# Order of score, value, turn and projection work within a step of three attentions of a decoder kernel

## Chip, cores and metric

One Trainium2 chip, one core. The metric is the device time of one execution in microseconds (us), the median of several runs; lower is better.

## What is computed

A decoder of four layers works on x of 16 sequences, 128 tokens, 256 features, all in f32. Each layer adds an attention-like, a cross-attention-like and a feed-forward part to x. Three of the attentions are touched by the change: `l1a` (layer 1, causal self-attention), `l2fa` (the self-attention without mask inside layer 2's feed-forward part) and `l3x` (layer 3, cross-attention to a context, with a time bias, 4 key and value heads). They all have 16 query heads of 16 features. The one of layer 3, cut to what matters:

```python
q = (query @ Wq).reshape(B, S, H, D).transpose(0, 2, 1, 3)
k = (key @ Wk).reshape(B, S, G, D).transpose(0, 2, 1, 3)
v = (value @ Wv).reshape(B, S, G, D).transpose(0, 2, 1, 3)
scores = jnp.einsum('bhqd,bhkd->bhqk', q, k_rep) * SCALE
...
scores = scores + time_bias[:, None, :, :]
...
w = jax.nn.softmax(scores, axis=-1)
out = jnp.einsum('bhqk,bhkd->bhqd', w, v_rep)
return out.transpose(0, 2, 1, 3).reshape(B, S, E) @ Wo
```

## The kernel before

Every attention of the kernel is built by one function, `attention_block` (from L393 on). Its plan says which mask it has, how many heads, and where keys and values come from. The order of work on each engine is written out by hand; the engines meet through semaphores.

**Steps.** The work is cut into T = 32 steps t: step t handles 8 of the 16 heads (HEADS = 8, in two groups of UNIT = 4) of one sequence, so two steps make a sequence and four (PER = 4) make a pair of sequences. What belongs to one step is spread over the following ones: its scores come in step t, its exponentials and maxima too, its sums one step later, the turning (transposing) of its probabilities TURN = 3 steps later, its value products VALUES = 4 steps later, and the output projection of a whole sequence in the step after the second half's value products.

**Projections.** Beside this, the projections for the next pair run as "fills" of two PSUM banks, `proj`: y (the turned rows of x), c (the turned context, in cross-attentions), k, q, v and, for each sequence, o (the output projection). A table `at[(t, sec)]` deals them out over the steps and over three sections of each step. In l1a and l2fa the first step of a round of four has y, the second k, the third q, the fourth v, all in section 0, and o in section 1 of the first and third. In l3x the first has c in section 0 and o and y in section 2, the second k and the third q in section 1 (with o in section 2 of the third), the fourth v in section 0. I call the four steps r0 to r3. A fill waits until its bank has been emptied of the fill two before it.

**TensorE** (the loop at L726 to L741). `score(t)` (L659) multiplies queries with a wide key tile in which each head has its own columns; it waits until the first group's exponentials of step t-1 are done, because there are three score banks for two in use. In l1a and l0x a mask matmul stands ahead of it (L675). `turn(t - TURN)` (L693) makes eight transposes, and waits for the probabilities and for the copies of the half turned a step before. `values(t - VALUES)` (L702) makes eight products of 32 columns each, and waits for both copies of its turned probabilities (`copied[0]` by VectorE, `copied[1]` by ScalarE) and for the copy out of the value products before it. Where `adjacent` (L415) is set, as it is for l2a and l0x, the values follow directly behind the scores; elsewhere, so in the three attentions of the change, they stand between sections 1 and 2. The turn stands between sections 0 and 1.

**VectorE** (L910 to L944), in each step: two row maxima (L904, or L901 with the addend in l3x), the sums of the step before (L921) and their reciprocals (L927), the emptying of section 0's fills, the copy of the first turned half (L937), the emptying of sections 1 and 2. Emptying k takes eight operations (L809) in l1a, l0x and l2fa. Emptying o adds it to the residual and takes that sequence's statistics (L856 to L862).

**ScalarE** (L1081 to L1112), in each step: four exponentials (L1070), the emptying of section 0, four exponentials (in l2fa and l3x the second four also sum, L1072), the copy of the second turned half (L1096), section 1, the copy out of the value products (L1079; directly behind the first four exponentials where `adjacent`), section 2. It empties y, c and part of q, k, v; in l3x also k, in eight operations (L1029).

**GpSimd** multiplies the probabilities by the reciprocals (L994) and normalises the next rows. **SyncE** loads the context and masks.

After step T a "head" is made: the first four sequences' rows of the next block are normalised by VectorE (L279), turned by TensorE (L289) and copied (L299, L308), between the last turns and value products.

Of the kernel before, what the change touches and what calls it, by code (L numbers as in the profile page):

```python
# [389 lines left out]
UNIT = 4  # L390


def attention_block(chip, plan, w, prefetch, have_stats, leave_twice):  # L393
# [18 lines left out]
    VB = 3 if small or S == 1 else 2  # L412
    added = plan.mask == "timebias" or t_ in ("l2a",)
    between = added and not small and not ctxsrc
    adjacent = t_ in ("l2a", "l0x")  # L415
    SUMMED = UNIT if t_ in ("l3x", "l2fa") else HEADS


# [52 lines left out]
    with ExitStack() as scope:  # L471
# [101 lines left out]
        with nc.Block() as block:  # L573
# [29 lines left out]
            def _(pe):  # L603
# [122 lines left out]
                for t in range(T + VALUES + 2):  # L726
                    if t < T:
                        score(t)
                    if adjacent and 0 <= t - VALUES < T:
                        values(t - VALUES)  # L730
                    for x in at[(t, 0)]:
                        project(x)
                    if 0 <= t - TURN < T:
                        turn(t - TURN)
                    for x in at[(t, 1)]:
                        project(x)
                    if not adjacent and 0 <= t - VALUES < T:
                        values(t - VALUES)
                    for x in at[(t, 2)]:
                        project(x)  # L740
                    if t == T + 1 and head:  # L741
                        pe.wait_ge(exps_done, 2 * T)
                        head.turn(pe, scores)
# [25 lines left out]
            def _(dve):  # L769
# [119 lines left out]
                if plan.mask == "timebias":  # L889
                    dve.wait_ge(key_ready, 1)  # L890
                    biased(0)

                def row_max(t, a):
                    b = t // S
                    g, j = divmod(b, PAIR)
                    bank = scores[(2 * t + a) % 3][:, :].rearrange("p (i k) -> p i k", i=UNIT)
                    dve.wait_ge(scores_ready, 2 * t + a + 1)
                    if added:
                        addend = {"timebias": lambda: bias[:, b, :], "causal": lambda: chip.causal[:, :], "support": lambda: mask_b[:, g % 2, j, :]}[plan.mask]()
                        for i in range(UNIT):  # L900
                            op = dve.tensor_tensor_reduce(out=bank[:, i, :], in0=bank[:, i, :], in1=addend, scale=-1.0, scalar=FMAX, op0=ALU.add, op1=ALU.min,  # L901
                                                          accum_out=nmx[:, t % 2, a * UNIT + i:a * UNIT + i + 1])
                    else:
                        op = dve.tensor_reduce(nmx[:, t % 2, a * UNIT:(a + 1) * UNIT], bank, AX.X, ALU.max, negate=True)  # L904
                    if plan.mask == "support":
                        dve.drain()
                        op = dve.tensor_scalar(nmx[:, t % 2, a * UNIT:(a + 1) * UNIT], nmx[:, t % 2, a * UNIT:(a + 1) * UNIT], padcol[:, b:b + 1], None, ALU.min)
                    op.then_inc(max_ready, 1)

                for t in range(T + VALUES + 2):  # L910
                    if t < T:
                        row_max(t, 0)
                        if between:
                            for x in at[(t, 0)]:
                                if not by_scalar(x[1]):
                                    empty(x)
                        row_max(t, 1)
                    if 0 <= t - 1 < T:
                        u = t - 1
                        dve.wait_ge(exps_done, 2 * u + 2)  # L920
                        dve.tensor_reduce(rsum[:, u % 2, 0:SUMMED], p[:, u % (TURN + 1), 0:SUMMED, :], AX.X, ALU.add)  # L921
                        dve.drain()
                        if plan.mask == "support":
                            dve.wait_ge(pads_done, u + 1)
                            dve.scalar_tensor_tensor(out=rsum[:, u % 2, :], in0=padt[:, u % 2, :], scalar=npad[:, u // S:u // S + 1], in1=rsum[:, u % 2, :], op0=ALU.mult, op1=ALU.add)
                            dve.drain()
                        dve.reciprocal(rinv[:, u % (TURN + 1), :], rsum[:, u % 2, :]).then_inc(rinv_ready, 1)  # L927
                    if plan.mask == "keymask" and t % PER == 0 and t // PER + 1 < PAIRS:
                        make_valid(t // PER + 1)
                    for sec in range(3):  # L930
                        for x in at[(t, sec)]:
                            if not by_scalar(x[1]) and not (between and sec == 0 and t < T):
                                empty(x)
                        if sec == 0 and 0 <= t - TURN < T:
                            u = t - TURN
                            dve.wait_ge(probsT_ready, 2 * u + 1)
                            dve.tensor_copy(pT[:, u % 2, 0:UNIT, :], probsT[0][:, :].rearrange("p (i q) -> p i q", i=UNIT)).then_inc(copied[0], 1)  # L937
                    if plan.mask == "timebias" and 1 <= t < NB // 4:
                        biased(t)
                    if t == T and head:  # L940
# [61 lines left out]
            def _(act):  # L1002
# [78 lines left out]
                for t in range(T + VALUES + 2):  # L1081
# [2 lines left out]
                    if adjacent and 0 <= t - VALUES < T:  # L1084
                        copy_out(t - VALUES)
                    for x in at[(t, 0)]:
                        if by_scalar(x[1]):
                            empty(x)
                    if t < T:
                        exps(t, 1)  # L1090
# [2 lines left out]
                    if 0 <= t - TURN < T:  # L1093
                        u = t - TURN
                        act.wait_ge(probsT_ready, 2 * u + 2)
                        act.copy(pT[:, u % 2, UNIT:HEADS, :], probsT[1][:, :].rearrange("p (i q) -> p i q", i=UNIT)).then_inc(copied[1], 1)  # L1096
                    for x in at[(t, 1)]:
                        if by_scalar(x[1]):
                            empty(x)
                    if not adjacent and 0 <= t - VALUES < T:  # L1100
# [3312 lines left out]
```

## Time and profile before

| | |
|---|---|
| Median of 3 runs | 2851.52 us (2845.75 to 2853.3) |
| Profiled execution, its own time | 2852.58 us |
| Its span | 2850.7 us |
| Mean granted TensorE clock | 0.949 |
| TensorE busy | 2524.3 us, 89% of the span |
| VectorE busy | 1729.2 us, 61% |
| ScalarE busy | 1257.8 us, 44% |
| GpSimd busy | 856.2 us, 30% |
| First and last scores of l1a | 582.6 and 737.8 us |
| First and last scores of l2fa | 1721.5 and 1864.8 us |
| First and last scores of l3x | 2268.8 and 2416.1 us |

The time of an execution lies about 2 us above its span, from the first to the last instruction. The shares are means over the whole kernel; a single attention looks different, so the rows below are taken inside single rounds of four steps. In the timeline, PE is TensorE, DVE VectorE, ACT ScalarE and POOL GpSimd. A PE row's length has the modelled end of its last matmul in it, so the time that a group takes from TensorE's queue is read from its start to the start of the next group.

### The profile page before, as it was taken

The numbers are of one execution on the slowest core, as the hardware profiler recorded it, in microseconds if no ns is written. First come the engines' busy times: TensorE is split into PE (matmuls) and PEld (weight loads), VectorE is DVE, ScalarE is ACT, GpSimd is POOL, SyncE is SP. The second block draws the span as 40 slices with busy tenths as digits, with TensorE's granted clock in tenths as the row PEclk, the third lists the DMA queues.
The fourth block names the chain that finished last, engine by engine and source line by source line (L and its number), as shares of the span: only waits on it lengthen the run. The fifth ranks groups of instructions, "written<-read, shape, count | busy, mean of one in ns | idle before, by whom it ended". The sixth has DMA issues, their size and how long they took to land. (4 is left out here: it accounts for less than half of the span.)

```text
span 2850.7 us, 49404 instructions
## 1 busy us (share of the span) xinstructions
PE 2524.3 (89%) x16337; PEld 1828.8 (64%) x16337; DVE 1729.2 (61%) x4957; ACT 1257.8 (44%) x3451; POOL 856.2 (30%) x687
## 2 busy tenths in 40 slices
PE   4998989989799889599998998969969899969997
PEld 2666765766544356477776776748956576449996
DVE  7875986588766644355564567973345588344443
ACT  2333664256455323444443445734432488324342
POOL 4533540045431044122221226631110044132222
PEclk8999999999899899799999999979989999989999
DMA  9001000000300333200001002051130300531110
GB/s 321 15 0 51 14 2 18 1 16 1 84 11 1 58 94 116 96 1 1 1 1 47 18 1 75 2 207 35 39 90 1 87 19 2 192 121 50 53 51 27
DMA packets 155271, 144.08 MB, mean 51 GB/s; under 512 B 62024, under 2 KB 139982, under 8 KB 154640
## 3 DMA queue, kind: packets, MB, share of 16 engines
q1 hardware_dynamic: 142880, 112.17, 13.6%
q0 software_dynamic: 10560, 27.19, 2.8%
q8 instruction: 137, 2.24, 0.3%
q10 hardware_dynamic: 1584, 1.57, 0.2%
q14 instruction: 110, 0.90, 0.1%
HBM read 99.70 MB, written 43.02 MB: 50 GB/s over the span
## 5 line engine op out<-in xcount | busy, mean ns | idle before, releaser
L994 POOL TENSOR_TENSOR room<-room 128x1024 f32<-128x1024 f32 x144 | 273.9, 1902 | 408.7 <-DVE room L927 408.5
L1473 PE MATMUL l3f_out<-room,Y 128*128 x624 | 141.1, 379 | 0.0
L921 DVE TENSOR_REDUCE room<-room 128x8 f32<-128x1024 f32 (+1 forms) x144 | 139.9, 972 | 1.0 <-ACT room L1072 0.8
L3645 DVE SCALAR_TENSOR_TENSOR room<-l1x_v,room 128x512 f32<-128x512 f32 x128 | 86.8, 685 | 65.5 <-ACT room L3791 65.2
L994 POOL TENSOR_TENSOR room<-room,Y 128x1024 f32<-128x1024 f32 x32 | 60.7, 1896 | 215.3 <-DVE Y L927 215.3
L1473 PEld LDWEIGHTS l3f_out<-room,Y 128*128 128x128 f32 x624 | 115.6, 190 | 14.2
L1070 ACT ACTIVATE room<-l2a_scores,Y 128x128 f32<-128x128 f32 x256 | 73.4, 375 | 96.6 <-DVE Y L901 96.6
L3791 ACT ACTIVATE room<-l1x_u 128x512 f32<-128x512 f32 x128 | 76.0, 598 | 76.0 <-PE l1x_v L3460 75.7
L1070 ACT ACTIVATE room<-l0x_scores,room 128x128 f32<-128x128 f32 x256 | 74.0, 390 | 55.0 <-DVE room L904 55.0
L1070 ACT ACTIVATE room<-l1a_scores,room 128x128 f32<-128x128 f32 x256 | 71.6, 387 | 59.4 <-DVE room L904 59.4
L626 PE MATMUL l2a_proj<-room 128*128 128x256 f32 x384 | 90.7, 384 | 0.0
L955 POOL MEMSET room<- 128x3072 f32 (+1 forms) x4 | 9.4, 2338 | 269.9 <-POOLq L144 269.9
L1775 DVE SCALAR_TENSOR_TENSOR Y<-Y,vecs 128x256 f32<-128x256 f32 x39 | 18.9, 485 | 116.6 <-DMA Y<-out,l3f_dest 116.6
L901 DVE CUSTOM_DVE_ANT_0 l2a_scores<-l2a_scores,causal 128x128 f32<-128x128 f32 x256 | 65.7, 323 | 33.0 <-PE l2a_scores L688 32.9
L1473 PE MATMUL l2fm_out<-room,Y 128*128 x368 | 83.1, 379 | 0.0
L1866 ACT COPY l3f_yn<-room 128x2048 f32 x39 | 74.5, 1911 | 16.4 <-DMA sorted_rows<-l3f_yn,l3f_place_i 16.0
L1463 PEld LDWEIGHTS l3f_hidden<-Y,l3f_yn 128*128 128x128 f32 x640 | 75.5, 196 | 5.8 <-DVE Y L1728 5.3
L1463 PE MATMUL l3f_hidden<-Y,l3f_yn 128*128 128x128 f32 x640 | 77.8, 281 | 1.2 <-DVE Y L1728 1.1
L626 PEld LDWEIGHTS l2a_proj<-room 128*128 128x128 f32 x384 | 70.5, 190 | 11.5 <-issue 3.1
L1911 POOL DMA_INDIRECT out<-Y,l3f_dest x39 | 39.1, 1002 | 127.5 <-DVE Y L1775 127.5
L1463 PEld LDWEIGHTS l3f_hiddenT<-Y,l3f_yn 128*128 128x128 f32 x608 | 69.7, 192 | 6.4 <-DVE Y L1728 5.8
L1473 PEld LDWEIGHTS l2fm_out<-room,Y 128*128 128x128 f32 x368 | 68.2, 190 | 8.4
(878 smaller groups left out, 6939.5 us busy)
## 6 DMA issues: line engine op xcount, KB each, us to landing
sorted_rows<-head SPq DMA_DIRECT2D x1, 16640.0 KB, 57.2
room<-in_L_ffn_w SPq DMA_DIRECT2D x16, 1024.0 KB, 13.3
room<-in_L_ffn_W SPq DMA_DIRECT2D x16, 1024.0 KB, 12.5
room<-in_ctx SPq DMA_DIRECT2D x32, 256.0 KB, 3.1
Y<-sorted_rows SPq DMA_DIRECT2D x62, 130.0 KB, 2.1
room<-sorted_rows SPq DMA_DIRECT2D x39, 130.0 KB, 2.1
room<-results SPq DMA_DIRECT2D x8, 512.0 KB, 7.4
room<-in_L_ffn_routed_w SPq DMA_DIRECT2D x4, 512.0 KB
```

What stands on the lines that cost most here:

```text
L626: mm = pe.matmul(bank[:, (c - i) * PT:(c - i + 1) * PT], w.v[kind][:, kc, c * P:(c + 1) * P], (y_of(g) if kind == "q" else c_of(g))[:, kc, ...
L901: op = dve.tensor_tensor_reduce(out=bank[:, i, :], in0=bank[:, i, :], in1=addend, scale=-1.0, scalar=FMAX, op0=ALU.add, op1=ALU.min, accum ...
L921: dve.tensor_reduce(rsum[:, u % 2, 0:SUMMED], p[:, u % (TURN + 1), 0:SUMMED, :], AX.X, ALU.add)
L994: pool.tensor_tensor(p[:, u % (TURN + 1), :, :], p[:, u % (TURN + 1), :, :], rinv[:, u % (TURN + 1), :].unsqueeze(2).to_broadcast([P, HEAD ...
L1070: op = act.activation(p[:, t % (TURN + 1), h, :], bank[:, i * P:(i + 1) * P], ACT.Exp, bias=nmx[:, t % 2, h:h + 1], scale=sign)
L1463: mm = pe.matmul(hidden[n % 2][a][:, q * P:(q + 1) * P], stage[:, n % 2, kc * F + f * P:kc * F + (f + 1) * P], rowsT[:, n % 2, kc, :], sta ...
L1473: mm = pe.matmul(obank[n % 2][:, 0:D], hT[:, n % 2, f, :], chip.room[:, bass.ds(at + (SLOT // 2 + f * D), D)], start=(f == 0), stop=(f == ...
L1775: op = dve.scalar_tensor_tensor(out=result[:, n % 2, :], in0=result[:, n % 2, :], scalar=gate[:, n % 2, 0:1], in1=so_far, op0=ALU.mult, op ...
L1866: act.copy(stage[:, n % 2, :], chip.room[:, bass.ds(at, KC * F)]).then_inc(staged, 1)
L1911: pool.indirect_dma_start(final_rows, bass.IndirectOffsetOnAxis(dest[:, n % DESTS:n % DESTS + 1], 0), result[:, n % 2, :], None, bounds_ch ...
L3645: dve.scalar_tensor_tensor(out=W[:, k % 2, p, :], in0=v_bank[n % 2][:, :], scalar=0.0, in1=W[:, k % 2, p, :], op0=ALU.max, op1=ALU.min).th ...
L3791: act.activation(W[:, k % 2, p, :], u_bank[n % 2][:, :], ACT.Relu).then_inc(u_ready, 1)
```

## The change

A new flag, `turn_first`, is set for l1a, l2fa and l3x, and sets `adjacent` for them. A step on TensorE is then: scores, value products, turn, and the fills of sections 0, 1 and 2. VectorE's copy of the first turned half becomes a small function, `copy_turned`; with the flag it stands behind the second row maxima and ahead of the sums. On ScalarE the copy out of the value products moves behind the first four exponentials, and the emptying of section 0 moves behind the copy of the second turned half. The other attentions keep their order.

```diff
--- before.py
+++ after.py
@@ -412,7 +412,8 @@
     VB = 3 if small or S == 1 else 2
     added = plan.mask == "timebias" or t_ in ("l2a",)
     between = added and not small and not ctxsrc
-    adjacent = t_ in ("l2a", "l0x")
+    turn_first = t_ in ("l1a", "l2fa", "l3x")
+    adjacent = turn_first or t_ in ("l2a", "l0x")
     SUMMED = UNIT if t_ in ("l3x", "l2fa") else HEADS
 
 
@@ -728,9 +729,11 @@
                         score(t)
                     if adjacent and 0 <= t - VALUES < T:
                         values(t - VALUES)
+                    if turn_first and 0 <= t - TURN < T:
+                        turn(t - TURN)
                     for x in at[(t, 0)]:
                         project(x)
-                    if 0 <= t - TURN < T:
+                    if not turn_first and 0 <= t - TURN < T:
                         turn(t - TURN)
                     for x in at[(t, 1)]:
                         project(x)
@@ -890,6 +893,10 @@
                     dve.wait_ge(key_ready, 1)
                     biased(0)
 
+                def copy_turned(u):
+                    dve.wait_ge(probsT_ready, 2 * u + 1)
+                    dve.tensor_copy(pT[:, u % 2, 0:UNIT, :], probsT[0][:, :].rearrange("p (i q) -> p i q", i=UNIT)).then_inc(copied[0], 1)
+
                 def row_max(t, a):
                     b = t // S
                     g, j = divmod(b, PAIR)
@@ -915,6 +922,8 @@
                                 if not by_scalar(x[1]):
                                     empty(x)
                         row_max(t, 1)
+                    if turn_first and 0 <= t - TURN < T:
+                        copy_turned(t - TURN)
                     if 0 <= t - 1 < T:
                         u = t - 1
                         dve.wait_ge(exps_done, 2 * u + 2)
@@ -931,10 +940,8 @@
                         for x in at[(t, sec)]:
                             if not by_scalar(x[1]) and not (between and sec == 0 and t < T):
                                 empty(x)
-                        if sec == 0 and 0 <= t - TURN < T:
-                            u = t - TURN
-                            dve.wait_ge(probsT_ready, 2 * u + 1)
-                            dve.tensor_copy(pT[:, u % 2, 0:UNIT, :], probsT[0][:, :].rearrange("p (i q) -> p i q", i=UNIT)).then_inc(copied[0], 1)
+                        if sec == 0 and not turn_first and 0 <= t - TURN < T:
+                            copy_turned(t - TURN)
                     if plan.mask == "timebias" and 1 <= t < NB // 4:
                         biased(t)
                     if t == T and head:
@@ -1084,7 +1091,7 @@
                     if adjacent and 0 <= t - VALUES < T:
                         copy_out(t - VALUES)
                     for x in at[(t, 0)]:
-                        if by_scalar(x[1]):
+                        if by_scalar(x[1]) and not turn_first:
                             empty(x)
                     if t < T:
                         exps(t, 1)
@@ -1094,7 +1101,7 @@
                         u = t - TURN
                         act.wait_ge(probsT_ready, 2 * u + 2)
                         act.copy(pT[:, u % 2, UNIT:HEADS, :], probsT[1][:, :].rearrange("p (i q) -> p i q", i=UNIT)).then_inc(copied[1], 1)
-                    for x in at[(t, 1)]:
+                    for x in (at[(t, 0)] if turn_first else []) + at[(t, 1)]:
                         if by_scalar(x[1]):
                             empty(x)
                     if not adjacent and 0 <= t - VALUES < T:
```

## Rows read from the trace of the kernel before

**Rows 1.** Busy time in one round of four steps: l0x, l1a, l2fa, l3x.

```profile
core 0: us, PE busy (x) PEld busy (x) DVE busy (x) ACT busy (x) POOL busy (x), PEclk, DMA share, GB/s
318.37:338.76 20.39, 20.38 (x177) 14.99 (x176) 18.97 (x38) 12.92 (x45) 10.78 (x8) 1.00 0.07 16
626.22:646.84 20.62, 20.48 (x173) 14.34 (x173) 18.74 (x37) 12.72 (x45) 10.85 (x8) 1.00 0.01 1
1783.45:1801.93 18.48, 18.33 (x168) 13.90 (x164) 16.62 (x37) 14.21 (x61) 12.90 (x10) 1.00 0.01 2
2331.98:2350.95 18.97, 18.14 (x170) 13.68 (x169) 15.99 (x88) 17.07 (x69) 9.67 (x7) 1.00 0.05 16
```

**Rows 2.** Timeline, l1a, TensorE in r2: start us, length us, engine, what.

```profile
652.88 1.99 PE L626 MATMUL l1a_proj<-room 128*128 128x256 f32 x8
...
655.01 1.07 PE L699 MATMUL l1a_probsT<-ident,room 128*128 128x128 f32 x8
...
655.91 1.03 PE L648 MATMUL l1a_proj<-room 128*128 128x256 f32 x4
...
656.87 0.64 PE L717 MATMUL l1a_out<-room 128*32 128x128 f32 x16
```

**Rows 3.** Timeline, l0x, from the end of r1 to the values of r3.

```profile
322.66 0.59 PE L675 MATMUL l0x_scores<-l0x_mask_b,ident_b 128*128 128x512 bf16 x2
...
322.87 3.71 DVE L809 TENSOR_SCALAR room<-l0x_proj,vecs,block_of 128x256 f32<-128x256 f32 x8
...
323.19 1.13 PE L681 MATMUL l0x_scores<-room 64*128 64x256 f32 x8
...
324.25 0.65 PE L717 MATMUL l0x_out<-room 128*32 128x128 f32 x16
...
325.76 1.03 PE L648 MATMUL l0x_proj<-room 128*128 128x256 f32 x4
...
326.50 1.27 DVE L904 TENSOR_REDUCE room<-l0x_scores 128x4 f32<-128x512 f32 x2
...
326.63 1.99 PE L626 MATMUL l0x_proj<-room 128*128 128x256 f32 x8
...
327.20 1.14 ACT L1070 ACTIVATE room<-l0x_scores,room 128x128 f32<-128x128 f32 x4 [4.13 <-DVE room L904]
...
328.37 1.18 ACT L1070 ACTIVATE room<-l0x_scores,room 128x128 f32<-128x128 f32 x4
...
328.46 0.59 PE L675 MATMUL l0x_scores<-l0x_mask_b,ident_b 128*128 128x512 bf16 x2
...
329.38 0.65 ACT L1096 COPY room<-l0x_probsT 128x512 f32<-128x512 f32 x1
...
330.12 0.64 PE L717 MATMUL l0x_out<-room 128*32 128x128 f32 x16
```

**Rows 4.** Timeline, l3x, TensorE and ScalarE from r1 to r3.

```profile
2337.14 3.10 ACT L1029 ACTIVATE room<-l3x_proj,block_of 128x256 f32<-128x256 f32 x8
...
2340.53 0.65 PE L717 MATMUL l3x_out<-room 128*32 128x128 f32 x16 [0.27 <-ACT room L1079]
...
2341.11 1.13 PE L648 MATMUL l3x_proj<-room 128*128 128x256 f32 x4
...
2342.17 1.14 PE L681 MATMUL l3x_scores<-room 64*128 64x256 f32 x8
...
2343.86 1.10 PE L634 MATMUL l3x_proj<-room 128*128 128x64 f32 x8 [0.56 <-ACT room L1041]
...
2344.49 1.14 ACT L1070 ACTIVATE room<-l3x_scores,room 128x128 f32<-128x128 f32 x4 [0.53 <-DVE room L901]
```

**Rows 5.** Timeline, l2fa: second exponentials, ScalarE's copy, VectorE's emptying of k.

```profile
1793.31 0.40 ACT L1072 ACTIVATE room<-l2fa_scores,room 128x128 f32<-128x128 f32 x1
...
1794.68 0.65 ACT L1096 COPY room<-l2fa_probsT 128x512 f32<-128x512 f32 x1
...
1805.18 3.65 DVE L809 TENSOR_SCALAR room<-l2fa_proj,vecs,block_of 128x256 f32<-128x256 f32 x8
```

**Rows 6.** Timeline, l1a, tail: VectorE's copy of a turned half.

```profile
748.29 0.68 DVE L937 COPY room<-l1a_probsT 128x512 f32<-128x512 f32 x1
```

## The prediction

> **What bounds the kernel now.** I read the windows first: one full round of four steps in each of the three attentions, and one of l0x, which already runs its value products directly behind the scores and is left as it is. A step is one half (8 of 16 heads) of one sequence, and four steps carry one projection round for the next pair of sequences. In l1a TensorE is busy 20.48 of 20.62 us, in l2fa 18.33 of 18.48, in l3x 18.14 of 18.97; the granted clock is 1.00 in all four [rows 1]. So TensorE's queue sets the pace, but VectorE is at 18.74 of 20.62 in l1a and ScalarE at 17.07 of 18.97 in l3x: neither has much room. What I then look for in the timelines is only two things: which pair of neighbours on TensorE's queue costs time, and how early each copy is ready that TensorE waits for.
>
> In l1a's third step the queue loses time to VectorE: the q fill begins at 652.88 and the turn behind it at 655.01, 2.13 us later [rows 2], where the same fill in l0x takes 326.63 to 328.46, 1.83 us [rows 3]. The turn waited for VectorE's copy of the half turned before, which stood behind the eight operations that empty the k fill. A second loss is the order itself: the output projection ahead of the values takes 655.91 to 656.87, 0.96 us [rows 2], and 0.87 ahead of another full-width fill (325.76 to 326.63) [rows 3].
>
> **The change in parts.** Nothing is added or removed: 32 steps in each attention, with the same matmuls, copies and DMAs; SP's and GpSimd's queues are as they were. On TensorE values(t-4) moves from behind the first or second group of projections to directly behind score(t), turn(t-3) follows it, and all fills come last. VectorE's copy of the turned half moves ahead of the sums and of the emptying; the change's description says "directly behind the sums", but in the diff it stands directly behind the row maxima, ahead of the sums. ScalarE copies the value products out between its two groups of exponentials, and empties all fills behind its copy of the turned half. Steps 0 to 2 have no turn or values, steps 28 to 31 no fills but the output projection, so the change acts on six full rounds (steps 4 to 27) of each attention, on four steps after them and on the tail.
>
> *Floor of TensorE, l1a.* l0x has the order wanted, the same mask matmul and one more fill, the context's four transposes, which I take at 0.49 us (as long as half an output projection's 0.87, and a little more). Its round is 20.39 us [rows 1]; less 0.49 that is 19.9. Both losses above are gone in it: 0.30 for the copy, some 0.1 a step for the values.
>
> *Does a copy come late in l1a?* This is what the new order risks: the k fill now comes last in its step, so VectorE empties it later, and values(t-4) needs, right behind the scores, copies that were made one step before instead of having a whole step of slack. I count from the start of step r1 (the one with k), by l0x's rows [rows 3]: mask 0.53 (322.66 to 323.19), scores 1.06 (to 324.25), values and turn 1.51 (to 325.76), k 1.8: 4.9, and VectorE starts at about 5.0 (in l0x it starts 0.21 behind the end of the fill, 322.87 against 322.66). The eight operations take 3.63 (to 326.50), so the row maxima of r2 start at 8.6; exponentials 0.70 later (327.20), 1.17 for four and the copy out (to 328.37), 1.01 for the other four (to 329.38), and values may start 0.74 behind the start of ScalarE's copy (330.12): 12.2. TensorE gets there at 4.9 + (0.53 + 1.06 + 1.51 + 1.83 + 0.87 = 5.8) + 1.59 = 12.3. So l1a just fits: 19.9 against 20.62, 0.7 a round, **-4.3 us** over six. Bounds: VectorE's 18.74 of busy time leaves only 1.2 a round free, so 0 if it uses that up in waits; -5.5 if the late fills also save the 0.1 that l0x pays where q is followed by the mask.
>
> *l2fa.* No mask: the floor is 19.9 less four times 0.53, and plus 0.09 in each step, because the scores (which use 64 rows) now follow full-width work: in l3x an output projection that stands between values and scores takes 1.06 (2341.11 to 2342.17) [rows 4], two such boundaries, against the 0.96 with one and the 0.87 with none. That gives 18.14. Here the copies do come late. ScalarE's second four exponentials also sum and take 1.37 us (1793.31 to the copy at 1794.68) [rows 5], not 1.01, and TensorE arrives earlier because there is no mask. From r1: 1.06 + 1.51 + 1.83 = 4.4, k emptied from 4.5 for 3.63, row maxima at 8.13, then 0.70 + 1.17 + 1.37 + 0.74 = 12.1. TensorE is ready for the values of r3 at 4.4 + (1.06 + 1.51 + 1.83 + 0.96 = 5.36) + 1.06 = 10.8. **Stall 1.3 us in every round**: 19.44 against 18.48, **+5.8 us** over six. Today this does not show, since k is filled before the turn (VectorE takes it up at 1805.18, 3.2 us into the step that starts at 1801.93) [rows 1, 5] and the values stand at the end of the step. Bounds: -2 (no stall) to +8 (a second stall of 0.4 where y is emptied).
>
> *l3x.* Floor: 18.14, plus 0.49 for the context, less 0.89 because its v fill is half as long (1.10 us against 1.99) [rows 4, 3]: 17.75. Two waits of today go: 0.27 for the copy out (2340.53) and 0.56 for ScalarE ahead of v (2343.86) [rows 4]. But k is emptied by ScalarE: exponentials begin 2.32 behind the scores' start (2342.17, 2344.49) [rows 4], then 1.17 + 1.37 + 0.5 for its copy = 5.3, k for 3.0 (the eight at 2337.14 take 3.10, the end of the last beside what follows) = 8.3, exponentials of r2 1.17 + 1.37 = 10.9, values at 11.6 where TensorE is ready at 10.8: 0.8 lost, and some 0.3 in the step behind it. 17.75 + 1.1 is 18.85; with the round's other overlaps I take 18.7 against 18.97, **-1.5 us** over six. Bounds: -7.3 (floor) to +3.
>
> *Last steps and tails.* In steps 28 to 31 the chain scores, maxima, exponentials, copy, values, turn closes in two steps; with l2fa's sums that is 0.5 us longer than today. In step 32 VectorE now waits for a turn that stands behind the values before it takes the last sums, and the rows of the next block's head wait for it; in l1a the copy at 748.29 [rows 6] already waits behind that work. I take 0.5 us each, bounds -0.5 and +2: **+1.5** and **+0.5**.
>
> **Sum.** -4.3 + 5.8 - 1.5 + 0.5 + 1.5 = +2.0. The profiled execution took 2852.58 us (span 2850.7); 2854.6 for one like it. The median of the three runs is 1.1 below that, so I predict 2853.5. Differences under 0.3% (8.6 us) can't be told from none with this kernel.
>
> A page of the Trainium skill bears on the order. "TensorEngine Tiling (Array Packing)", section Key Properties, says that a change of tiling mode drains TensorE. The trace has such a price: the 0.96 against 0.87 above. By the rule alone l1a has three changes of mode a step instead of four (full, 64 rows, 32 columns, full), l2fa three as before, and l3x one less in one step of four.
>
> **Rivals.**
> *A, the order on TensorE alone counts.* One boundary less in l1a at 0.09 (0.96 less 0.87) [rows 2, 3] for 29 steps, one in seven steps of l3x, no stall won or lost elsewhere: -3.2, 2848.3, no change that can be told. Against it speaks the late copy in l2fa, for it that 0.09 is plain in the rows. The skill's rule named above would have it so. Chance 0.12.
> *B, faster.* The copies are never late: every round runs at TensorE's floor, 19.9, 18.14 and 17.75, so -4.3, -2.0 and -7.3, 2838. It decides at ScalarE's copy in r2: it must start by 10.1 us after r1's start in l2fa where I count 11.4. For it: today TensorE waits for a copy in these rounds only 0.3 to 0.6 us at a time. Against it: the 3.63 of emptying k is one block that nothing passes. Chance 0.14.
> *C, slower.* VectorE's copy, now ahead of the sums, waits for a turn that is itself held behind the values. With 0.5 us of that in one step of each round, and VectorE's 1.2 free in l1a gone, l1a's round is 21.1 (+3.0), l2fa's 19.9 (+8.8), l3x's as today, and each tail costs 1.2 (+3.6): about +15, 2867. It decides where the turn's first half comes later than the end of the row maxima. By l0x's rows the first half is done some three quarters through the 1.51 us of values and turn, 2.7 after the mask, and the two maxima, 1.27 long, end near 3: close enough to be possible [rows 3]. Chance 0.16.
> *D, the copy is not where the description has it.* Behind the sums it would come later by one sum; l0x has it there, and its values in r3 start at 330.12 with ScalarE's copy ready at the same moment. That is under 0.1 us a round: it changes no number here. It is no case of its own.
>
> **How the numbers follow.** My forecast has 0.58: with A that is 0.70 for no change, of which 0.01 each goes to either side for its spread: faster 0.15, same 0.68, slower 0.17. The range of the forecast by its bounds is 2846 to 2861. To leave out no more than 2 in 10 it reaches into B and C: 2843 to 2864.
>
> **What would show it.** In the profile after: l1a's round near 19.9 with the wait of the turn for VectorE gone; l2fa's near 19.4 with a wait of over 1 us ahead of the values in one step of four, put down to ScalarE's or VectorE's copy; l3x's near 18.7 with two shorter ones, and the waits ahead of v and for the copy out gone; granted clock still 1.00. If l2fa's values never wait, B holds and my chain from k to the copy is wrong. If VectorE shows idle time ahead of its copy of the turned half, it is C.

## The result and the profile after

The changed kernel takes 2869.17 us in the median of five runs (2862.58 to 2873.74); the kernel before, in the same session, 2851.52 (2845.37 to 2855.61, five runs). The ratio is 1.0064, with a 95% interval of 1.0046 to 1.0081: 0.6% slower, outside the range that I gave. The one profiled execution took 2862.58 us (span 2860.8), the lowest of the five.

The busy time in one round of four steps, in the same order as in [rows 1], here of the changed kernel (stretch and its length, then busy us and instructions of each engine, granted clock, DMA):

```profile
core 0: us, PE busy (x) PEld busy (x) DVE busy (x) ACT busy (x) POOL busy (x), PEclk, DMA share, GB/s
319.40:339.79 20.39, 20.39 (x177) 14.99 (x176) 18.96 (x38) 12.88 (x45) 10.78 (x8) 1.00 0.07 16
626.62:646.53 19.91, 19.86 (x173) 14.49 (x172) 18.83 (x38) 12.48 (x44) 10.86 (x7) 1.00 0.00 1
1780.52:1800.06 19.54, 18.21 (x165) 13.82 (x164) 16.93 (x36) 14.21 (x61) 12.93 (x9) 1.00 0.01 2
2341.48:2362.09 20.61, 17.97 (x169) 13.79 (x168) 16.17 (x86) 17.09 (x67) 9.66 (x7) 1.00 0.05 14
```

l0x, which the change leaves alone, is the same to 0.01 us. l1a's round fell from 20.62 to 19.91, l2fa's rose from 18.48 to 19.54, and l3x's from 18.97 to 20.61. In both that rose TensorE does slightly less busy time than before and waits for the rest.

From trace to trace the same round of the same code repeats to some 0.04 us, while executions of one kernel differ by 10 us, so I judge by rounds, and by the time from the start of an attention's first fill to the end of its last one. The exception is l3x's first round, which took 19.35, 19.46 and 20.39 us in three traces of the old order.

| | before | after | difference | forecast |
|---|---|---|---|---|
| l1a, steps 4 to 27 | 123.2 | 119.0 | -4.2 | -4.3 |
| l2fa, steps 4 to 27 | 110.0 | 117.3 | +7.3 | +5.8 |
| l3x, steps 4 to 27 | 114.4 | 123.5 | +9.1 | -1.5 |
| first fill to last fill: l1a | 181.0 | 177.9 | -3.1 | |
| the same, l2fa | 167.2 | 178.8 | +11.6 | |
| the same, l3x | 182.1 | 191.0 | +8.8 | |

The last three rows sum to +17.3, and the medians differ by 17.7. The two profiled executions differ by 10 only because the untouched rest of the kernel took some 7 us less in the second.

**l2fa.** The timeline of the changed kernel from r1 to r3 (start us, length us, engine, line, what, and idle time before it; lines of other engines between them are left out):

```profile
1785.16 3.71 DVE L812 TENSOR_SCALAR room<-l2fa_proj,vecs,block_of 128x256 f32<-128x256 f32 x8 [0.61 <-PE l2fa_proj L627]
...
1788.78 1.27 DVE L911 TENSOR_REDUCE room<-l2fa_scores 128x4 f32<-128x512 f32 x2
...
1789.49 1.14 ACT L1077 ACTIVATE room<-l2fa_scores,room 128x128 f32<-128x128 f32 x4 [3.81 <-DVE room L911]
...
1790.69 1.13 PE L682 MATMUL l2fa_scores<-room 64*128 64x256 f32 x8 [0.32 <-ACT room L1077]
...
1792.03 0.64 ACT L1103 COPY room<-l2fa_probsT 128x512 f32<-128x512 f32 x1
...
1792.77 0.64 PE L718 MATMUL l2fa_out<-room 128*32 128x128 f32 x16 [0.95 <-issue]
```

k is emptied from 4.64 us after the start of its step (1780.52), row maxima at 8.26, ScalarE's copy at 11.51, values at 12.25. This is the chain of the forecast, where I had 4.5, 8.13, 11.4 and 12.1. ScalarE was idle for 3.81 us in front of its exponentials: not its load is the trouble but what it waits for. The scores of r3 wait 0.32 us and its values 0.95, together 1.27 where I had a stall of 1.3.

The first of the six rounds is another case. It has no output projection in r0, and in the kernel before it took 17.61 us for that. Now it takes 19.55 like the others: TensorE waits 0.93 us ahead of r1's values, which start 5.17 us behind the scores of r0 (1737.46 to 1742.63), with no emptying of k between them. r0 is only 3.10 us long there.

**l3x.** What I had not seen stands in r0:

```profile
2360.33 0.64 ACT L1103 COPY room<-l3x_probsT 128x512 f32<-128x512 f32 x1
2360.80 0.66 ACT L1027 COPY room<-l3x_proj 128x512 f32<-128x512 f32 x1
...
2361.51 0.66 PE L617 MATMUL l3x_proj<-ident,room 128*128 128x128 f32 x4 [1.36 <-ACT room L1027]
2362.09 1.14 PE L682 MATMUL l3x_scores<-room 64*128 64x256 f32 x8
2362.20 0.59 ACT L1025 COPY room<-l3x_proj 128x512 f32<-128x512 f32 x1 [0.75 <-PE l3x_proj L617]
```

r0 has three fills, c, o and y, for two banks. y needs the bank of c. ScalarE now empties c (L1027) behind its second exponentials and its copy, and the three fills have moved together, so TensorE stands for 1.36 us ahead of y (L617). In the same round it also waits ahead of the values in two steps:

```profile
PEld l3x_proj L617 <- ACT room L1027: 1.8, 1, 1.8
PE l3x_proj L617 <- ACT room L1027: 1.4, 1, 1.4
PE l3x_out L718 <- issue: 0.7, 1, 0.7
PE l3x_out L718 <- ACT room L1103: 0.6, 1, 0.6
```

(In the round from 2355.49 to 2376.10: engine, line and what it waited for; us in all, times, longest.) The two waits of before, for the copy out and ahead of v [rows 4], are gone.

**The tail of l2fa** grew from 16.1 us (start of the last scores to the end of the last fill) to 19.7. ScalarE's copy, TensorE's values and VectorE's copy and sums in step 32, of the changed kernel:

```profile
1870.71 0.64 ACT L1103 COPY room<-l2fa_probsT 128x512 f32<-128x512 f32 x1
...
1871.60 0.64 PE L718 MATMUL l2fa_out<-room 128*32 128x128 f32 x16 [2.76 <-ACT room L1103]
1872.18 1.09 PE L700 MATMUL l2fa_probsT<-ident,room 128*128 128x128 f32 x8
...
1872.87 0.69 DVE L898 COPY room<-l2fa_probsT 128x512 f32<-128x512 f32 x1 [2.67 <-PE l2fa_probsT L700]
...
1873.48 0.68 DVE L930 TENSOR_REDUCE room<-room 128x4 f32<-128x512 f32 x1
```

and the same sums in the kernel before:

```profile
1868.35 0.63 ACT L1096 COPY room<-l2fa_probsT 128x512 f32<-128x512 f32 x1
1868.53 0.69 DVE L921 TENSOR_REDUCE room<-room 128x4 f32<-128x512 f32 x1 [0.59 <-ACT room L1072]
```

They stood 0.18 us behind the start of ScalarE's copy and stand 2.77 behind it now. TensorE's mean granted clock in this tail was 1.00 before and 0.91 after, and its busy time, for the same work, 12.18 us and 13.69: 1.5 of the 3.6 us go with the clock.

### The profile page after: what moved, and what is told of

Its sections match the earlier page's. It is cut to its first block and busy times, and to the rows that moved or that the text cites. A ratio compares the mean times of both kernels' runs of the same rounds, so it can differ in the third digit from the quotient of the medians.

```text
span 2860.8 us, 49404 instructions
## 1 busy us (share of the span) xinstructions
PE 2507.7 (88%) x16337; PEld 1824.1 (64%) x16337; DVE 1735.5 (61%) x4957; ACT 1254.1 (44%) x3451; POOL 856.1 (30%) x687
## 5 line engine op out<-in xcount | busy, mean ns | idle before, releaser
L1782 DVE SCALAR_TENSOR_TENSOR Y<-Y,vecs 128x256 f32<-128x256 f32 x39 | 18.9, 484 | 104.0 <-DMA Y<-out,l3f_dest 104.0
L908 DVE CUSTOM_DVE_ANT_0 l3x_scores<-l3x_scores,room 128x128 f32<-128x128 f32 x256 | 64.9, 325 | 22.3 <-PE l3x_scores L682 21.9
```

Source lines behind the costliest of these rows:

```text
L1782: op = dve.scalar_tensor_tensor(out=result[:, n % 2, :], in0=result[:, n % 2, :], scalar=gate[:, n % 2, 0:1], in1=so_far, op0=ALU.mult, op ...
```

## The experiments

Times of whole kernels are compared with the kernel before on the same chip; one chip was 13 us slower for the kernel before. Experiments 3 to 7, 9 and 10 were executed once each, so I judge them by their rounds and not by their whole times.

**1. The new order in l1a alone.**

```diff
-    turn_first = t_ in ("l1a", "l2fa", "l3x")
+    turn_first = t_ in ("l1a",)
```

> The new order in l1a alone; l2fa and l3x as in the kernel before. Theory 1 (each attention pays for its own late copy or late bank, independently): l1a takes 178.0 us from its first fill to its last, as in the changed kernel (181.0 before), a round of four steps 19.9; l2fa and l3x are back at 167.3 and 182.2; the whole kernel 3 us under the kernel before, 2848. Theory 2 (the loss is something common to the three, such as the order of VectorE's queue or TensorE's clock): l1a's gain comes and goes with the others, and the total is not under the kernel before.

l1a: rounds of 19.91 or 19.92, but for the first (19.27) and the fifth (20.09), 179.5 us from first fill to last (one early step went slower, in l0x too). l2fa is back at 167.3, l3x at 181.0. Twelve runs: median 2861.56 against 2864.61, ratio 0.9993 (0.9981 to 1.0005). The attentions pay independently, as theory 1 has it. The 3 us cannot be told from none in the whole kernel's time.

**2. c emptied between the exponentials in l3x.**

```diff
                     for x in at[(t, 0)]:
-                        if by_scalar(x[1]) and not turn_first:
+                        if by_scalar(x[1]) and (not turn_first or t_ == "l3x"):
                             empty(x)
...
-                    for x in (at[(t, 0)] if turn_first else []) + at[(t, 1)]:
+                    for x in (at[(t, 0)] if turn_first and t_ != "l3x" else []) + at[(t, 1)]:
```

> The changed kernel, but in l3x ScalarE empties the fill of section 0 (the turned context, c) between its two groups of exponentials, as before the change. Theory 1 (l3x loses because TensorE's y fill waits for the bank that c leaves, 1.36 us in the first step of each round): that wait goes, l3x's round falls from 20.61 to 19.2 to 19.4, the attention from 191.0 to about 182 to 183, the kernel by about 8.5 against the changed one, to some 2860. Theory 2 (l3x loses through the late emptying of k and the late copies that values wait for, as predicted): the round stays at 20.3 or more.

A round of l3x, and TensorE's waits in it:

```profile
2383.32:2402.37 19.05, 17.78 (x170) 13.79 (x169) 16.17 (x87) 17.09 (x68) 9.62 (x6) 1.00 0.01 2
```

```profile
PE l3x_out L718 <- issue: 0.7, 2, 0.5
PE l3x_out L718 <- ACT room L1103: 0.5, 1, 0.5
```

The wait ahead of y is gone, and the last two rounds are 19.05 and 19.06; the first took 20.82, the three behind it 19.53, 19.39 and 19.23. l3x takes 183.8 us instead of 191.0, a little over the 182 to 183 that was expected: the bank of c cost 1.56 us in a late round, and 6.4 over all six. Ratio to the kernel before 1.0025 (1.001 to 1.004), against 1.0064 for the whole change. Theory 1 holds, with a rest of 1.2 us of waits ahead of the values.

**3. VectorE's copy behind the sums**, where the description has it: the two lines of the call stand behind the reciprocal.

```diff
                         row_max(t, 1)
-                    if turn_first and 0 <= t - TURN < T:
-                        copy_turned(t - TURN)
                     if 0 <= t - 1 < T:
...
+                    if turn_first and 0 <= t - TURN < T:
+                        copy_turned(t - TURN)
```

> The changed kernel with VectorE's copy of the turned half behind the sums and reciprocals instead of ahead of them. Theory 1 (the place of this copy matters little inside the rounds, and something in the tail, where the last sums wait behind a turn that waits for the values): rounds of l1a, l2fa and l3x stay at 19.9, 19.5 and 20.6 within 0.15; each tail (step 32 on) is shorter by 1 to 2 us, so 3 to 5 us in all. Theory 2 (VectorE waits for the turn in its new place, and this makes the loss): rounds of l2fa and l3x fall by 0.5 us or more.

Rounds of 19.92, 19.56 and 20.65: nothing moved, and theory 2 falls. Theory 1's 3 to 5 us in the tails did not come either. The tails (last scores to last fill), with TensorE's busy time and granted clock in them:

| | changed kernel | copy behind the sums |
|---|---|---|
| l1a | 18.66, busy 13.69, clock 0.91 | 19.88, busy 15.25, clock 0.83 |
| l2fa | 19.69, busy 13.69, clock 0.91 | 17.11, busy 12.07, clock 1.00 |
| l3x | 19.30, busy 13.73, clock 0.91 | 18.96, busy 13.69, clock 0.91 |

Most of what moves here goes with the clock. In five more runs with the copy ahead of the sums and a clock of 0.91 l2fa's tail took 18.5 to 19.0 us; in experiment 7, which has this copy behind the sums too, it took 18.2 at 0.91. So with like clocks the copy's place is worth 0.3 to 0.8 us in l2fa (1.5 against the changed kernel's own trace) and 0.3 in l3x; whether it also brings the clock down is open.

**4. In l2fa, r3 in the old order** on all engines (scores, v, turn, values; TensorE's part shown).

```diff
+    old_order = lambda t: t_ in ('l2fa',) and t % PER in (3,)
...
-                    if adjacent and 0 <= t - VALUES < T:
+                    old = old_order(t)
+                    if adjacent and not old and 0 <= t - VALUES < T:
                         values(t - VALUES)
-                    if turn_first and 0 <= t - TURN < T:
+                    if turn_first and not old and 0 <= t - TURN < T:
                         turn(t - TURN)
...
```

> The changed kernel, but in l2fa the fourth step of each round (the one with v) keeps the old order on all engines: scores, v, turn, values, copy out late. Theory 1 (l2fa loses because the values of this step wait for copies made late behind the emptying of k): the wait of 0.95 us and more goes, the round falls from 19.54 to 18.3 to 18.5, the attention from 178.8 to about 171 to 172. Theory 2 (it loses by the order itself, the scores of 64 rows behind full-width fills, or by late copies in every step): the round stays over 19.2.

The round rose to 20.30, where theory 1 had 18.3 to 18.5. TensorE's waits in one of them:

```profile
PE l2fa_proj L636 <- ACT room L1049: 1.7, 1, 1.7
PE l2fa_scores L683 <- ACT room L1080: 0.3, 1, 0.3
```

v, now directly behind the scores, waits 1.7 us for its bank, which q holds until ScalarE is behind its late exponentials. A miss that neither theory had: it tells them apart no better than before, but it is the wait for a bank once more, in another attention.

**5. Half of k's emptying left out in l2fa.**

```diff
                     if kind == "k" and small:
-                        for c in range(i, i + per_bank):
+                        for c in range(i, i + (1 if t_ == "l2fa" and g >= 2 else per_bank)):
```

> The changed kernel, but in l2fa VectorE empties only four of the eight parts of each k fill from the third pair of sequences on, so that heads 8 to 15 keep the keys of an earlier pair: that part of the work is left out. Theory 1 (l2fa's loss is the chain from the late k fill over VectorE's 3.6 us of emptying to the copies that the values wait for): the chain is 1.8 us shorter, more than the wait of about 1.3 us, so l2fa's round falls from 19.55 to 18.1 to 18.3, under the 18.48 of the kernel before. Theory 2 (the loss is in the order on TensorE, or in copies that are late in every step): the round falls by less than 0.5.

```profile
1811.23:1829.37 18.14, 18.13 (x166) 13.82 (x165) 15.19 (x32) 14.31 (x62) 12.86 (x10) 1.00 0.01 2
```

18.14 in all six rounds. In five of them TensorE is busy for all but 0.01 to 0.07 us of it. The matmuls and their order are unchanged; only VectorE's block of 3.6 us is 1.8 shorter. So in these five l2fa's whole loss is that block in front of the copies, and 18.14 is the floor that I had worked out from l0x. In the first, which has one output projection less, TensorE is busy for 17.21 us and the wait of 0.93 ahead of r1's values is still there: that one is not k's.

**6. k emptied by ScalarE in l2fa.**

```diff
-                return kind == "q" or (kind == "k" and plan.mask == "timebias")
+                return kind == "q" or (kind == "k" and (plan.mask == "timebias" or t_ == "l2fa"))
```

> The changed kernel, but in l2fa ScalarE empties the k fills, as it does in l3x; VectorE is free of them. Theory 1, by the same chain: ScalarE is through with its copy at 5.4 us after the start of the step with k, with k at 8.3, its exponentials and copy bring the values of r3 to 11.6 instead of 12.2, where TensorE is ready at 10.9: round 18.8 to 19.0 instead of 19.55. Theory 2 (VectorE is what is overloaded in this attention): with 3.6 us of 17 taken from it the round falls to TensorE's floor, 18.2.

The round is 19.24, above the 18.8 to 19.0 that the chain gave, and far from 18.2: with VectorE 3.5 us a round less busy (13.50 against 17.00), the values still wait 0.9 us in one step. VectorE's load is not the bound; that the same block on another engine stands in the same chain fits this, and the chain came out 0.2 to 0.4 short.

**7. The early values alone**: values and copy out directly behind the scores, turn and copies where they were.

```diff
-    turn_first = t_ in ("l1a", "l2fa", "l3x")
-    adjacent = turn_first or t_ in ("l2a", "l0x")
+    turn_first = False
+    adjacent = t_ in ("l1a", "l2fa", "l3x", "l2a", "l0x")
```

> One part of the change alone: in the three attentions the value products and their copy out stand directly behind the scores, but the turn stays behind the fills of section 0, VectorE's copy behind the emptying of section 0, and ScalarE empties section 0 between its exponentials. Theory 1 (the values can stand there only if the copies come early): in l1a and l2fa the copy of r1 now stands behind the emptying of k and the values of r2 wait some 2 us for it: rounds of 21.5 or more in l1a (19.91 with the whole change) and 20.3 or more in l2fa (19.55); in l3x, where ScalarE empties k and the c fill leaves its bank early, 19.0 to 19.4 (20.62). Theory 2 (the early values are the gain and the early turn is the loss): l1a stays at 20.0 or less, l2fa falls to 18.5.

Rounds: l1a 23.7 to 24.0 (21.80 in the first), l2fa 23.4 to 23.5 (21.85 in two), l3x 18.9 to 19.6. The whole kernel took 2902.89 us. One round each of l1a, l2fa and l3x, and TensorE around the wait in l1a:

```profile
695.64:719.62 23.98, 21.58 (x173) 15.83 (x173) 19.12 (x37) 12.82 (x44) 10.85 (x8) 0.93 0.00 1
1855.71:1879.24 23.53, 20.03 (x165) 15.13 (x165) 16.98 (x37) 14.61 (x61) 12.88 (x10) 0.93 0.01 2
2418.05:2437.02 18.97, 17.82 (x169) 13.83 (x168) 16.06 (x88) 17.12 (x70) 9.70 (x7) 1.00 0.01 2
```

```profile
704.91 1.14 PE L682 MATMUL l1a_scores<-room 64*128 64x256 f32 x8
708.44 0.71 PE L718 MATMUL l1a_out<-room 128*32 128x128 f32 x16 [2.40 <-DVE room L898]
709.08 3.35 PE L627 MATMUL l1a_proj<-room 128*128 128x256 f32 x7
```

The wait of 2.4 us is the one expected: VectorE's copy behind the emptying of k. (The last row ends with its window; the whole fill, eight matmuls, takes 3.57 us.) So in l1a the early values alone only lose, and need the early turn and the early copy; the early turn alone was not tried, the early copy alone only in l2fa (experiment 11). In l3x the early values alone are as good as before the change.

**8. l1a alone, and there VectorE's copy behind the sums from step 32 on.**

```diff
-                    if turn_first and 0 <= t - TURN < T:
+                    if turn_first and t < T and 0 <= t - TURN < T:
                         copy_turned(t - TURN)
...
+                    if turn_first and t >= T and 0 <= t - TURN < T:
+                        copy_turned(t - TURN)
```

> The new order in l1a alone, and there VectorE's copy of the turned half behind the sums from step 32 on. Theory 1 (the last sums need not wait for a turn that stands behind the values): l1a's loop stays at 150.25 to 151.5 us, its tail is 0.5 to 1.2 us shorter than the 18.4 to 18.7 of the same order without this; the kernel 3 to 4 us under the kernel before, ratio 0.9985 to 0.9995. Theory 2 (the tail is set by the head's rows and the granted clock): the tail stays within 0.3 us.

l1a's tail is 18.15 us against 18.34 with experiment 1, both at a clock of 0.91; ratio 1.0001 (0.9989 to 1.0013). Theory 2's 0.3 us holds here; experiment 1's 0.9993 and this 1.0001 are one result, no change that can be told.

**9. l3x with c between the exponentials and half of k's emptying left out on ScalarE** (experiment 2's edit and this one).

```diff
                     elif kind == "k" and small:
-                        for c in range(i, i + per_bank):
+                        for c in range(i, i + (1 if t_ == "l3x" and g >= 2 else per_bank)):
```

> The changed kernel with two edits in l3x: ScalarE empties c between its two groups of exponentials, as before, and from the third pair on it empties only four of the eight parts of each k fill (heads 8 to 15 keep an earlier pair's keys: that part of the work is left out). Theory 1 (behind the bank of c, l3x has a second cost of the same kind as l2fa: copies made late behind the emptying of k, now on ScalarE): the round falls from 19.06 to 17.6 to 18.2, near TensorE's floor of 17.6 to 17.8. Theory 2 (with the bank wait gone l3x is at its floor, and 19.06 is TensorE's own work in this order): it stays over 18.8.

The round stays at 19.07 (from the third on; the first took 22.68). Theory 1 is wrong here, and so is theory 2's floor: TensorE still waits, elsewhere. The timeline from r3's scores to r0's values:

```profile
2357.05 1.13 PE L682 MATMUL l3x_scores<-room 64*128 64x256 f32 x8
...
2358.27 0.28 DVE L908 CUSTOM_DVE_ANT_0 l3x_scores<-l3x_scores,room 128x128 f32<-128x128 f32 x1
...
2359.38 1.14 ACT L1077 ACTIVATE room<-l3x_scores,room 128x128 f32<-128x128 f32 x4 [1.60 <-DVE room L908]
...
2360.67 1.13 PE L682 MATMUL l3x_scores<-room 64*128 64x256 f32 x8
...
2361.93 0.64 ACT L1103 COPY room<-l3x_probsT 128x512 f32<-128x512 f32 x1
...
2362.82 0.65 PE L718 MATMUL l3x_out<-room 128*32 128x128 f32 x16 [1.01 <-ACT room L1103]
```

The wait ahead of r3's values is gone and that ahead of r0's has grown to 1.01 us. ScalarE is on time with k. From r3's scores (2357.05) over maxima, exponentials and copy to the values of the next step it takes 5.77 us, and r3, with its short v fill, is only 3.62 long with 1.06 of scores behind it. So the late k decides in which of the two steps TensorE waits, and not how long in both together. It is the wait of l2fa's first round once more.

**10. l3x with c between the exponentials, and VectorE sums all heads.**

```diff
-    SUMMED = UNIT if t_ in ("l3x", "l2fa") else HEADS
+    SUMMED = UNIT if t_ in ("l2fa",) else HEADS
```

> The changed kernel, c emptied between the exponentials in l3x, and there VectorE sums all eight heads, so that ScalarE's second four exponentials take 1.0 us instead of 1.4; the result is the same. Theory 1 (with values directly behind scores, each step of l3x must be at least as long as the chain from its scores over row maxima, exponentials and ScalarE's copy to the next values, 5.6 to 5.8 us less the 1.06 of the next scores, so that short steps are padded to 4.6): the chain is 0.37 shorter in every step, and the round falls from 19.06 to 18.3 to 18.7. Theory 2 (VectorE, busy 16.2 of 19, becomes the bound when it takes over the sums): the round stays at 19.0 or rises.

The last three rounds are 18.85 to 18.87 (the first took 23.75), 0.2 less than 19.06: between the theories. The chain is shorter, but VectorE, now 17.97 of 18.85 busy, takes back part of it, and a wait of 0.2 us for c's bank returns. That a short step is padded up to the chain fits this and experiment 9; how the 1.2 us divide is open.

**11. What the experiments point to**: the new order where it pays, and the two waits of TensorE in the other two shortened in the old order. In l2fa VectorE copies ahead of emptying k in r1; in l3x the v fill stands behind the turn, so that its bank is free.

```diff
-    turn_first = t_ in ("l1a", "l2fa", "l3x")
+    turn_first = t_ in ("l1a",)
...
-... if n * 3 * PER // len(body) == r * 3 + sec and ...
+... if n * 3 * PER // len(body) + (t_ == "l3x" and f[0] == "v") == r * 3 + sec and ...
...
+                    early_copy = t_ == "l2fa" and t % PER == 1 and 0 <= t - TURN < T
+                    if early_copy:
+                        copy_turned(t - TURN)
...
-                        if sec == 0 and not turn_first and 0 <= t - TURN < T:
+                        if sec == 0 and not turn_first and not early_copy and 0 <= t - TURN < T:
                             copy_turned(t - TURN)
```

> The new order in l1a alone, and two small edits in the old order of the others: in l2fa, in the step with k, VectorE copies the turned half ahead of emptying k (the turn of the next step no longer waits for it), and in l3x the v fill stands behind the turn instead of directly behind the scores (its bank is free by then). Theory 1 (waits of TensorE for a late copy or a late bank are what is left to win, and each is worth what the trace shows): l1a's round 19.91, l2fa's 18.1 to 18.2 instead of 18.48, l3x's 18.3 to 18.5 instead of 18.97; l1a 178 to 179.5 us, l2fa 165.5, l3x 178 to 179; the kernel 7 to 9 us under the kernel before, ratio 0.9965 to 0.998. Theory 2 (such waits move on to the next instruction): l2fa and l3x stay within 0.1 of 18.48 and 18.97 a round, the ratio at 0.999 or more.

```profile
1817.66:1835.80 18.14, 18.14 (x169) 13.98 (x165) 16.64 (x38) 14.15 (x62) 12.89 (x10) 1.00 0.01 2
2364.99:2383.65 18.66, 18.30 (x169) 13.75 (x169) 15.86 (x87) 16.99 (x69) 9.63 (x6) 1.00 0.01 2
```

l1a 19.91, l2fa 18.14, l3x 18.66 a round (18.3 to 18.5 was forecast). l2fa takes 166.1 us and l3x 180.6 (165.5 and 178 to 179 were forecast). Eleven runs: 2844.6 against 2852.47 us, ratio 0.9972 (0.9958 to 0.9986). It beats both kernels, the changed one by 0.9% if the two ratios are divided.

## Why the prediction was wrong

**l1a: right.** "19.9 against 20.62", by the round of l0x less the context; measured 19.91, and -4.2 for -4.3. "12.2 against 12.3" was close: in the round from 641.61 r3's values start 12.28 us after r1 (646.01 to 658.29), 0.13 later than directly behind the scores.

**l2fa: right in mechanism, small in size.** I had 19.44 and +5.8; it is 19.54 and +7.3. Experiment 5 shows the chain and the floor of 18.14 to be as worked out. What was missing: the first of the six rounds took 17.61 before, not 18.48, and lost 1.9 instead of 1.1 us, because its short r0 is stretched by the chain from r0's scores to r1's values. I had followed that chain only behind k.

**l3x: the step that failed.** I had -1.5; it is +9.1. "17.75 + 1.1 is 18.85; with the round's other overlaps I take 18.7". I counted when ScalarE is through with k and with its copies, and not when it is through with c, though the change moves that very operation behind the second exponentials, and though a fill waits until its bank has been emptied of the fill two before it. With three fills in r0 and all of them together at the end of the step, y follows c too soon. That is 1.56 us in a late round (experiment 2). Without it the round is 19.06, still 0.4 over my 18.7; leaving out half of k does not shorten it, so the late k of my chain does not set it; the trace of experiment 9 shows a short step stretched to the chain of 5.77 us instead. l3x's rounds make 10.6 of the 15 us by which the forecast of +2.0 fell short.

**Last steps and tails: +2.0 forecast.** In the loop's last steps l2fa lost 0.7 and l3x 0.5. l2fa's tail lost 3.6 where I had 0.5 and a bound of 2; l1a's lost 1.1, l3x's gained 1.0. The order of the waits was as I had it, but I had not followed the chain of copy, values, turn, copy and sums step by step, and I had no term for the clock. In l2fa's tail the clock makes 1.5 of the 3.6. l3x's gain is the clock as well: its tail of before had 0.83 (20.27 us), the one after 0.91 (19.30), and two traces of the old order at 0.91 took 18.76 and 18.85. Like against like, l3x's tail lost 0.5.

**The rivals.** C, slower by 15, came near in size and not in cause: VectorE waits for the turn for 0.3 us in l2fa's round, and its copy's place changes no round (experiment 3). That also bears out D: whether the copy stands ahead of the sums or behind them does not matter inside the loop. B falls with l2fa and l3x; experiment 5 shows its price where the copies come in time. A falls too: the order on TensorE alone does not decide. Its 0.09 us a change of mode fits l1a's steps: r0 and r1 fell by 0.10 and 0.15 us, r2 by 0.43, of which I had given 0.30 to the copy, and r3, whose values now come 0.13 late, by 0.02. That is small beside the waits of 0.9 to 1.4 us. The rule in the Trainium skill's "TensorEngine Tiling (Array Packing)", section Key Properties, that a change of mode drains TensorE, agrees with the trace so far; no run here changes the modes alone. A slip stands in A's count: l3x has fills in section 2 in two steps of four (r0 and r2), not in one, so that A comes to -3.9 instead of -3.2.

## What to carry to other kernels

When an order is changed for several users of one function, work the whole chain out for each, and for every fill of a shared bank ask who empties the one two before, and when: moving one engine's emptying behind its other work is a change to the producer's queue. Work placed directly behind its predecessor needs copies a whole step earlier. A long block ahead of those copies then has a price, as k's emptying has in l2fa; and even without one, a step shorter than the chain from its scores to the next values (5.2 us in l2fa's first round, 5.8 in l3x) is stretched to it. Where whole executions scatter by 10 us, a round that repeats to 0.04 us tells edits apart that the total cannot; compare tails only with the granted clock beside them.

## What the runs showed of the hardware

A wait can cost more than its length, and the length alone does not tell whether it will. In experiment 7 TensorE stood for 2.40 us ahead of l1a's values, and the fill behind them took 3.57 us where the one ahead of them took 1.99 (701.68 in the same trace). The round's granted clock was 0.93, so for part of it the lower of the two levels, 1.2 GHz, was granted, and TensorE was busy for 21.58 us, against 19.86 in the changed kernel's round. The waits of 0.95 and 1.36 us in l2fa and l3x left the clock at 1.00.

But in l2fa of the same trace the same wait has two outcomes, in one round and in the next:

```profile
1823.44 0.65 PE L718 MATMUL l2fa_out<-room 128*32 128x128 f32 x16 [2.46 <-DVE room L898]
1824.01 1.99 PE L627 MATMUL l2fa_proj<-room 128*128 128x256 f32 x8
...
1845.28 0.90 PE L718 MATMUL l2fa_out<-room 128*32 128x128 f32 x16 [2.46 <-DVE room L898]
1846.12 3.37 PE L627 MATMUL l2fa_proj<-room 128*128 128x256 f32 x8
```

The first of these rounds had a clock of 1.00 and took 21.85 us, the second 0.93 and 23.48: the clock alone is worth 1.6 us there. What decides between the two no run shows. In the tails much the same work kept TensorE busy for 12.1 to 12.2 us at a granted clock of 1.00, for 13.5 to 13.9 at 0.90 or 0.91, and for 14.8 to 15.5 at 0.82 or 0.83.
